# Half of the keys kept as differences to the other half, so that their scores are added into banks that already hold the row maximum

## The reference

```
x = x + attention(layernorm(x))      # 16 heads of 64, rotary positions on q and k, 1024 tokens
x = x + ffn(layernorm(x))            # 128 -> 352 -> 128, silu gate, blockwise FP4 quantise/dequantise

scores = einsum('bhid,bhjd->bhij', rotate(q), rotate(k)) * 64 ** -0.5
probs  = softmax(scores)             # over all 1024 keys j
out    = einsum('bhij,bhjd->bhid', probs, v)   ->  reshape  ->  @ w_out + b_out
```

## Time and profile before

| | |
|---|---|
| median of the runs | 1718.77 us |
| profiled execution | 1719.78 us, of it 1718.0 us from first to last instruction |
| TensorE busy | 1605.0 us (93%) |
| VectorE busy | 1180.9 us (69%) |
| ScalarE busy | 722.2 us (42%) |
| GpSimd busy | 1294.3 us (75%) |
| mean granted TensorE clock | 0.979 of full speed |

### The profile page before, as it was taken

One profiled execution on the slowest core, in us unless ns is written; L12 is line 12 of the kernel. 1 busy time (PEld: TensorE's weight loads), 2 busy tenths in 40 slices (PEclk: granted clock), 3 DMA queues, 4 the chain that ended last, 5 costly groups with the idle time before them and its releaser, 6 DMA issues.

```text
span 1718.0 us, 26114 instructions
## 1 busy us (share of the span) xinstructions
PE 1605.0 (93%) x10025; PEld 863.4 (50%) x10025; DVE 1180.9 (69%) x1440; ACT 722.2 (42%) x941; POOL 1294.3 (75%) x729
## 2 busy tenths in 40 slices
PE   3899999999999999999999999999999999997666
PEld 1455555555555555555545555555555545554454
DVE  4877776666667677766667767766667777654676
ACT  1244444544444544544444445444444534443222
POOL 4478888777778878887777878797777788865674
PEclk9799999999999999999999999999999999998888
DMA  4111111111111111111111111111111111100000
GB/s 123 42 38 33 44 44 43 38 45 44 40 35 35 44 33 44 44 36 44 45 44 40 26 44 36 40 44 39 42 45 44 40 36 34 27 16 21 13 13 25
DMA packets 69194, 67.12 MB, mean 39 GB/s; under 512 B 26512, under 2 KB 52432, under 8 KB 69072
## 3 DMA queue, kind: packets, MB, share of 16 engines
q1 hardware_dynamic: 69072, 65.46, 15.2%
HBM read 29.25 MB, written 2.62 MB: 19 GB/s over the span
## 4 chain that ended last, share of the span: by engine, by line
PE 83%; DVE 13%; POOL 1%; issue 1%; ACT 1%; DMA 0%; DVEq 0%; POOLq 0%
PE po L1059 27%; PE st L1047 24%; PE mx L1099 9%; PE ms L1082 8%; PE ms L1070 4%; PE ms L1115 4%; PE ms L1124 4%; DVE negmax L800 3%; DVE first_sum L822 2%; DVE max_rows L814 1%; PE ms L1106 1%; PE mx L1183 1%; DVE probs L756 1%; PE st L1183 1%; DVE amax L750 1%
## 5 line engine op out<-in xcount | busy, mean ns | idle before, releaser
L800 DVE TENSOR_REDUCE negmax<-mx 128x2 f32<-128x1024 f32 x504 | 615.6, 1221 | 376.4 <-PE mx L1099 376.4
L599 ACT ACTIVATE probs<-st 128x1024 f32<-128x1024 f32 x512 | 497.8, 1023 | 533.6 <-PE st L1047 533.6
L352 POOL TENSOR_TENSOR psum_keys<-psum_keys,probs 128x1024 f32<-128x1024 f32 x256 | 607.4, 2373 | 127.4 <-ACT probs L599 109.3
L1059 PE MATMUL po<-probs,v 128*64 128x512 f32 x2048 | 495.7, 605 | 0.0
L1047 PE MATMUL st<-heads 64*128 64x512 f32 x3072 | 440.0, 391 | 0.0
L1047 PEld LDWEIGHTS st<-heads 64*128 64x128 f32 x3072 | 289.9, 185 | 58.4 <-issue 2.4
L1099 PE MATMUL mx<-heads 64*128 64x512 f32 x1008 | 230.1, 452 | 29.7 <-DVE negmax L800 29.5
L1059 PEld LDWEIGHTS po<-probs,v 128*64 128x64 f32 x2048 | 124.2, 136 | 256.2 <-issue 147.0
L352 POOL TENSOR_TENSOR psum_keys<-probs 128x1024 f32<-128x1024 f32 x64 | 151.7, 2370 | 87.1 <-ACT probs L599 87.0
L1047 PE MATMUL st<-max_rows,one_rows 64*128 64x512 f32 x1024 | 201.9, 389 | 0.0
L1099 PEld LDWEIGHTS mx<-heads 64*128 64x128 f32 x1008 | 94.8, 184 | 186.3 <-issue 117.3
(11 more groups left out here) (144 smaller groups left out, 1237.0 us busy)
## 6 DMA issues: line engine op xcount, KB each, us to landing
kq<-sin_part SPq DMA_DIRECT2D x256, 128.0 KB, 2.4
rsum<-recips SPq DMA_DIRECT2D x128, 128.0 KB, 2.9
wqkv<-in_L_attn_w_qkv_dram SPq DMA_DIRECT2D x32, 192.0 KB, 2.8
resid<-in_L_attn_x_dram SPq DMA_DIRECT2D x4, 512.0 KB, 8.3
wout<-in_L_attn_w_out_dram SPq DMA_DIRECT2D x32, 64.0 KB, 2.6
out_dram<-resid SPq DMA_DIRECT2D x8, 256.0 KB, 2.3
sums<-sums_kept SPq DMA_DIRECT2D x64, 4.0 KB
spread<-sums SPq DMA_DIRECT2D x64, 4.0 KB, 1.5
```

Source lines behind the costliest of these rows:

```text
L352: nc.gpsimd.tensor_tensor(psum_keys[:, c], first, probs[:, (STEPS * P + i) % RING], ALU.add)\
L599: nc.scalar.activation(probs[:, step_n % RING], st[step_n % 2][:, :], ACT.Exp, scale=SCALE)\
L800: nc.vector.tensor_reduce(negmax[:, t // HALF, :, t % HALF, half], banks[:, :], AX.X, ALU.max, negate=True)\
L1059: last = mm(po[HD * a:HD * a + HD, :], v[:, P % 2, jt, HD * a:HD * a + HD], probs[:, step_n % RING, a], start=(jt == 0), stop=(jt == JT - 1))
```

## The change

The rotated keys of tokens 0 to 511 are kept as they are, those of tokens 512 to 1023 as the difference to the key 512 tokens before. GpSimd makes the difference with one more instruction per pair. The key tiles are taken in the order 0, 1, 4, 5, 2, 3, 6, 7, so a tile of the second half comes two steps behind its partner of the first half and meets the same `st` bank. Its three terms are added to what stands there (the scores of the partner, the maximum already in them), and the fourth term is not issued. The maxima do the same: the product of the first half of the keys comes first, that of the differences is added to it. For the maxima of pair 0 the banks are dealt out anew (`max_unit`), and their first columns are gathered after product 9 instead of 7. On VectorE, `first_keys` now stands ahead of `spread_maxima`.

```diff
+KEY_ORDER = (0, 1, 4, 5, 2, 3, 6, 7)
+    key_rows = kq[:, :].rearrange("p a n -> p (a n)")[:, CH:CH + TOKENS]
+    rotary_out = [key_rows, raw[1]]
+    def max_unit(N, u):
+        if N == 0 and u < 12:
+            return (mx, st[0], st[1])[u % 3], 3 * (u // 6) + u % 3, u % 6 // 3
+        return mx, u // 2, u % 2
+    def key_at(tile):
+        return bass.ts((tile + HALF) % JT, PART)
...
         def rope_add(L, s):
-            nc.gpsimd.tensor_tensor(raw[s], raw[s], swp[s], ALU.add).then_inc(rotated, 1)
+            add = nc.gpsimd.tensor_tensor(raw[s], raw[s], swp[s], ALU.add)
+            if s == 1:
+                add.then_inc(rotated, 1)
+            else:
+                add.then_inc(keys_rotated, 1)
+                pool.wait_ge(keys_rotated, L + 1)
+                nc.gpsimd.tensor_tensor(key_rows[:, 0:CH], raw[0][:, CH:TOKENS], raw[0][:, 0:CH], ALU.subtract)\
+                  .then_inc(rotated, 1)
...
-            dve.wait_ge(mx_free, 16 * N + 8 * c + 8)
+            dve.wait_ge(mx_free, 16 * N + (16 if c else 10 if N == 0 else 8))
...
                     if kind == "K":
                         rope_parts(X, u)
-                    if kind == "B":
-                        spread_maxima(X, u)
                     if kind == "O" and present(P):
                         accumulate(X, u)
                 if present(P) and d in (1, 3, 5, 6):
                     first_keys(P, d // HALF, int(d in (3, 6)))
+                for kind, X, u in units_at(P, d):
+                    if kind == "B":
+                        spread_maxima(X, u)
...
-            terms = ((k_lo[:, keys], q_hi[:, queries]), (k_hi[:, keys], q_hi[:, queries]),
-                     (k_hi[:, keys], q_lo[:, queries]), (one_rows[:, :], max_rows[:, queries]))
+            terms = [(k_lo[:, keys], q_hi[:, queries]), (k_hi[:, keys], q_hi[:, queries]),
+                     (k_hi[:, keys], q_lo[:, queries])]
+            if tile < HALF:
+                terms += [(one_rows[:, :], max_rows[:, queries])]
...
-                    last = mm(st[step_n % 2][:, a], stationary[rows], moving[rows], start=(n == 0), stop=(n == 3))
+                    last = mm(st[step_n % 2][:, a], stationary[rows], moving[rows], start=(n == 0 and tile < HALF),
+                              stop=(n == len(terms) - 1), skip_group_check=(tile >= HALF))
...
-                          heads[rows, N % SETS, 0, 0, bass.ts(half, CH)], start=True, stop=True)
+                          heads[rows, N % SETS, 0, 0, bass.ts(1 - half, CH)], start=(half == 0), stop=True,
+                          skip_group_check=(half == 1))
```

More of the change, by code:

```diff
@@ L148, in block_program @@
     cos_done, swap_in = sem("cos_done"), [sem("swap_k_in"), sem("swap_q_in")]
+    keys_rotated = sem("keys_rotated")
     rotated, hi_done, lo_done = sem("rotated"), sem("hi_done"), sem("lo_done")
@@ L482, in rope_add @@
             pool.wait_ge(swap_in[s], 64 * L + 64)
-            nc.gpsimd.tensor_tensor(raw[s], raw[s], swp[s], ALU.add).then_inc(rotated, 1)
+            add = nc.gpsimd.tensor_tensor(raw[s], raw[s], swp[s], ALU.add)
[6 more added lines that the diff above has]
+                  .then_inc(rotated, 1)
         def rope_lo(L, s):
             pool.wait_ge(hi_done, 2 * L + s + 1)
-            nc.gpsimd.tensor_tensor(heads[:, L % SETS, s, 1], raw[s], heads[:, L % SETS, s, 0].bitcast(F32), ALU.subtract)\
+            nc.gpsimd.tensor_tensor(heads[:, L % SETS, s, 1], rotary_out[s], heads[:, L % SETS, s, 0].bitcast(F32), ALU.subtract)\
               .then_inc(lo_done, 1)
@@ L621, in hi @@
             wait(act, st_ps, STEPS * (L - SETS + 1))
-            nc.scalar.activation(heads[:, L % SETS, s, 0], raw[s], ACT.Copy).then_inc(hi_done, 1)
+            nc.scalar.activation(heads[:, L % SETS, s, 0], rotary_out[s], ACT.Copy).then_inc(hi_done, 1)
         def pair(P):
@@ L796, in row_maxima @@
         def row_maxima(N, u):
-            t, half = u // 2, u % 2
+            banks, t, half = max_unit(N, u)
             dve.wait_ge(mx_full, 16 * N + u + 1)
-            banks = (mx, st[0], st[1])[u % 3] if N == 0 and u < 12 else mx
             nc.vector.tensor_reduce(negmax[:, t // HALF, :, t % HALF, half], banks[:, :], AX.X, ALU.max, negate=True)\
@@ L855, in pair @@
                         row_maxima(N, u)
-                        if u in (7, 15):
-                            max_columns(N, u // 8)
+                        if u in (9 if N == 0 else 7, 15):
+                            max_columns(N, u // 15)
                 for kind, X, u in units_at(P, d):
@@ L1040, in scores @@
             (k_hi, k_lo), (q_hi, q_lo) = ([heads[:, P % SETS, s, part] for part in range(2)] for s in range(2))
-            keys, queries = bass.ts(jt, PART), bass.ts(c, CH)
-            terms = ((k_lo[:, keys], q_hi[:, queries]), (k_hi[:, keys], q_hi[:, queries]),
-                     (k_hi[:, keys], q_lo[:, queries]), (one_rows[:, :], max_rows[:, queries]))
+            tile = KEY_ORDER[jt]
+            keys, queries = key_at(tile), bass.ts(c, CH)
+            terms = [(k_lo[:, keys], q_hi[:, queries]), (k_hi[:, keys], q_hi[:, queries]),
+                     (k_hi[:, keys], q_lo[:, queries])]
+            if tile < HALF:
+                terms += [(one_rows[:, :], max_rows[:, queries])]
             for n, (stationary, moving) in enumerate(terms):
@@ L1058, in times_v @@
             for a in range(2):
-                last = mm(po[HD * a:HD * a + HD, :], v[:, P % 2, jt, HD * a:HD * a + HD],
+                last = mm(po[HD * a:HD * a + HD, :], v[:, P % 2, KEY_ORDER[jt], HD * a:HD * a + HD],
                           probs[:, step_n % RING, a], start=(jt == 0), stop=(jt == JT - 1))
@@ L1085, in max_scores @@
         def max_scores(N, u):
-            t, half = u // 2, u % 2
-            banks = mx
+            banks, t, half = max_unit(N, u)
             if N == 0 and u < 12:
-                banks = (mx, st[0], st[1])[u % 3]
                 wait(pe, mx_free, u - 2)
```

## The result

The changed kernel takes 1665.11 us (median of 4 runs, 1664.75 to 1665.33) against 1718.99 us (4 runs): a ratio of 0.9684 with a 95% interval of 0.9672 to 0.9697. The forecast was 1661.5, in a range of 1649 to 1680. The gain is 53.9 us where 57.3 were forecast.

The account below looks back on a forecast made before the run. TensorE was taken as the bound, busy 93% of the span. 31 x 1.84 = 57.0, plus 1.2, minus 0.4 and 0.5, gave 57.3 us off: median 1661.5 us, range 1649 to 1680.

Parts of the forecast that it names:

- The key step: In a stage, 0.42 us lie between reduction end and second maxima product; removing matmuls takes 0.46 us from that gap.
- the four stages: Stages 1, 3, 5 and 7, which lose matmuls: gains of 0.28, 0.10, 0.28 and 1.18 us, 1.84 a pair.
- One sign: Second maxima product waits for the reduction three to four times a pair, at 0.2 to 0.3 us of TensorE's idle.
- The start-up: Before pair 0's scores: later gathering leaves the maxima transpose no longer hidden behind reductions, about 0.5 us lost.
- The pairs: 31 pairs gain 1.84 us each; pair 0 gains some 0.4 less, the last pair adds 1.2.
- The restart: In a stage whose second maxima product waits, the unit comes 0.47 us behind the end of VectorE's reduction.
- rival 1: Waiting product's weight load is issued early enough, so it costs 0.10 us less in four stages: 1649 us; chance 0.12.
- Rival 2: Reduction so late in stages 1, 3 and 5 that only the moved `first_keys` counts: 1682 us; chance 0.16.
- Rival 3: Short TensorE holes lower the clock; one stage a pair gives 1817 us; with other losses, 0.03 slower, 0.01 no difference.
- Rival 4: No handshake limit: all 0.46 in four stages and 1.08 us of present waiting go, 1629 us; chance 0.02.
- The subtraction on GpSimd: Once per pair before the key addition, 1.29 us, 41 us of work; costed at nothing, with 5.5 us of cover left.
- The last pair: No maxima from stage 2 on: gains 0.28 + 0.46 + 0.46 = 1.2 us; its stage 7 gives nothing.

Follow-up runs that it names:

- the kernel with six subtractions: Changed kernel with GpSimd's subtraction issued six times instead of once per pair, same result each time: 1735.76 us.
- the half-width reduction: Changed kernel with VectorE's reduction of each maxima product reading only 256 of 512 columns of each head: 1626.70 us.
- the three other orders tried here: Changed kernel with second maxima product behind the unit, 1738.92 us; that with VectorE's order too, 1696.86; regrouped start-up with first product moved forward, 1672.10.
- the kernel with the three-quarter reduction: Changed kernel with VectorE's reduction of each maxima product reading only 384 of 512 columns of each head: 1632.30 us.

## Why the prediction was right, and where it was off

The time and the mechanism were right. The key step was that the 0.42 us of slack between reduction and second product would be used up by the 0.46 taken out. In the pair from which it was worked out it came out to hundredths (forecast in brackets): stage 1 at 6.17 (6.16), stage 5 at 6.20 (6.20), stage 3 at 5.34 (5.33), and stage 7, with its batch transpose, 1.17 shorter (1.18). Over pairs 1 to 30 the four stages gain 0.25, 0.09, 0.24 and 1.17, where 0.28, 0.10, 0.28 and 1.18 were forecast. Three kernels show it from different sides: a shorter reduction gives 36.5 us back in the pairs, it does so mostly at a threshold, and where nothing waits the missing matmuls are worth 56.4. The stages 0, 2, 4 and 6 kept their length within 0.04 us, the clock stayed at 1.00, and in no wait between 100 and 1450 us did TensorE wait for GpSimd. One sign did not show as described: the waits come four times a pair, but not as 0.2 to 0.3 us of idle TensorE each.

Where 57.3 - 54.6 = 2.7 us of the span went, by the stretches of both traces:

- *The start-up* was sized at 0.5 us, from the transpose alone, and it was 1.65: this is the most mis-sized term of the sum. 1.3 of it came back with another order of the products, so that much is the later gathering. The other 0.35 can't be told from the clock, which was 0.91 between 60 and 80 us before the change and 0.83 after it.
- *The pairs*: 57.0 gained, 57.8 forecast (31 x 1.84 - 0.4 + 1.2). From pair 1 to pair 30 it is 1.80 a pair, and pair 0 gained 1.75.
- *The feed-forward layer*: 151.0 us instead of 150.3 in the profiled executions. In the traces of the experiments it is between 148.4 and 150.3. I have no cause, and one execution each can't tell it from spread.

The restart was taken at 0.47 from the one place that showed it; that held to 0.01 (0.48 in stages 1 and 7), and rival 1 (cheap restart) falls. Rival 2 (the handshake eats all) falls with stages 1 and 5. Rival 3 (the clock) falls: it was 1.00 from 100 to 1400 us. The Trainium skill says in "TensorE: Matmul & The Clock Gate" that frequent short idles between groups of matmuls can throw the clock back and forth; this stands in the section "A second HAM failure mode: psum-queue depth-cycling" and not in the one that the prediction names. The trace of the changed kernel does not agree, with its four short waits a pair at clock 1.00. In the kernel with six subtractions the clock did fall, behind 6 of 29 waits of up to 3.6 us. Rival 4 (pure TensorE time) was sized right, 1.84 + 1.08 = 2.92 us a pair: that is what pairs 1 to 30 lose with the half-width reduction (47.30 to 44.38), and rightly it was given almost nothing with the full one. The subtraction on GpSimd was hidden, as said. The last pair gained 1.2, as said (from its first product to the feed-forward layer 38.89 us instead of 40.10).

## What to carry to other kernels

Before counting what removed instructions save, find who hands a buffer back inside the gap they leave, and compare the gap with that engine's own duration. Here 0.46 us were taken out of 0.42 us of slack, and the waits that followed hold back 34 us that a shorter reduction gives. Look as well at the order on the other engine: to fill the idle time in front of a wait with work that stood behind it gave 35 of the 54 us. When a buffer is handed over in both directions, moving one side alone may not help: none of the three other orders tried here did, and only a shorter reader gave the time back. A second pair of banks for the maxima was not tried.

## What the runs showed of the hardware that I had not expected

- In the kernel with the three-quarter reduction, a product whose weight load alone was late, while the product itself started when due, still delayed what follows by 0.12 us (0.44 instead of 0.32 from product to unit).
- The same matmuls in another order take longer: a maxima product moved between the probabilities times v cost about 0.25 us more than in front of the scores. Four of them cost 1.01 us a pair, where the waits that they removed had cost 0.74.
- Adding into PSUM banks that hold a result from two steps before took no longer than starting them anew: 1468.6 us for the pairs against 1469.2.
- One idle time of TensorE of 1.86 us was followed by matmuls at half clock (1.48 us for six instead of 0.86), another of 2.83 us in the same kernel was not; idle times of 0.8 us once a pair, in the kernel before, never were between 100 and 1480 us.
